# Attention and LoRA feed-forward kernel: the last tile's second half cut into two quarters, and new instruction orders on all engines

## What is computed

```
def fake_quant(x, s, z):                       # to bytes and back
    return (clip(round(x / s + z), 0, 255) - z) * s
x = x + fake_quant(layernorm(x)) @ fake_quant(ctx)
y = layernorm(x)
weights, selected = top_k(y @ gate_w.T, 2)     # of 8 experts
w_full = one_hot(selected) weighted by softmax(weights)
low = einsum(y, lora_A)                        # 8 experts x rank 16
x = x + y @ base_w.T + base_b + 2.0 * einsum(low, lora_B, w_full)
```

## Time and profile before

| | |
|---|---|
| median of three executions | 171.46 us |
| the profiled execution | 171.14 us |
| span of its trace | 168.9 us |
| TensorE matmuls | 801, busy 159.1 us (94%) |
| VectorE, ScalarE, GpSimd busy | 119.2, 91.2, 18.4 us |
| granted TensorE clock, mean | 0.999 of full speed |

### The profile page before, as it was taken

One profiled execution on the slowest core, in us unless ns is written; L12 is line 12 of the kernel. 1 busy time (PEld: TensorE's weight loads), 2 busy tenths in 40 slices (PEclk: granted clock), 3 DMA queues, 4 the chain that ended last, 5 costly groups with the idle time before them and its releaser, 6 DMA issues.

```text
span 168.9 us, 2344 instructions
## 1 busy us (share of the span) xinstructions
PE 159.1 (94%) x801; PEld 119.6 (71%) x801; DVE 119.2 (71%) x290; ACT 91.2 (54%) x140; POOL 18.4 (11%) x40
## 2 busy tenths in 40 slices
PE   5787999999699999999999999999999999999992
PEld 1243435698588888878888767877888888888881
DVE  4887899996699989998799777964388171540212
ACT  3479999758931556804547687437729536000000
POOL 3132222002003000002200230004004000000000
PEclk9999999999999999999999999999999999999999
DMA  4999999999999923303480999994994992300033
GB/s 106 389 417 409 411 408 377 272 339 387 287 349 297 194 95 66 124 0 63 92 157 20 154 192 161 284 247 75 208 157 82 177 276 87 120 8 0 2 124 124
DMA packets 22187, 32.69 MB, mean 193 GB/s; under 512 B 13856, under 2 KB 13856, under 8 KB 22176
## 3 DMA queue, kind: packets, MB, share of 16 engines
q1 hardware_dynamic: 20016, 25.20, 46.2%
q0 software_dynamic: 2016, 7.34, 23.8%
q10 hardware_dynamic: 144, 0.00, 0.0%
HBM read 22.05 MB, written 4.19 MB: 155 GB/s over the span
## 4 chain that ended last, share of the span: by engine, by line
PE 72%; DMA 18%; SPq 4%; ACT 2%; issue 1%; DVE 1%; ACTq 0%
PE ps_even L1051 26%; PE ps_odd L1051 21%; DMA w_raw<-in_w_t 13%; PE ps_att L996 8%; DMA ring<-in_ctx 5%; PE ps_g L1032 5%; PE ps_g L1035 2%; SPq L250 1%; PE ps_t L977 1%; PE ps_even L1094 1%; PE ps_odd L1094 1%; PE ps_even L1093 1%; PE ps_even L1092 1%; PE ps_odd L1093 1%; PE ps_odd L1092 1%
## 5 line engine op out<-in xcount | busy, mean ns | idle before, releaser
L1051 PE MATMUL ps_even<-w_hi,yt 128*128 128x512 f32 x128 | 38.0, 395 | 0.0
L1051 PE MATMUL ps_odd<-w_hi,yt 128*128 128x512 f32 x128 | 37.4, 403 | 0.0
L1051 PEld LDWEIGHTS ps_odd<-w_hi,yt 128*128 128x128 f32 x128 | 24.0, 188 | 5.9 <-issue 0.2
L996 PE MATMUL ps_att<-c,c1t 128*128 128x512 f16 x96 | 27.4, 382 | 0.3 <-DVE c L705 0.3
L1051 PEld LDWEIGHTS ps_even<-w_hi,yt 128*128 128x128 f32 x128 | 23.4, 188 | 4.8
L1032 PE MATMUL ps_g<-ag,yt 128*128 128x272 f32 x64 | 20.8, 364 | 1.6 <-DVE yt L743 1.6
L1051 PE MATMUL ps_even<-w_lo,yt 128*128 128x512 f32 x64 | 20.6, 392 | 0.0
L1051 PE MATMUL ps_odd<-w_lo,yt 128*128 128x512 f32 x64 | 19.9, 394 | 0.0
L1032 PEld LDWEIGHTS ps_g<-ag,yt 128*128 128x128 f32 x64 | 12.1, 189 | 4.6 <-issue 2.0
L435 ACT ACTIVATE qc<-ring,q_in,q_rec 128x1024 uint16<-128x1024 f32 x11 | 13.4, 1234 | 2.1 <-DVE c L705 1.4
L1051 PEld LDWEIGHTS ps_even<-w_lo,yt 128*128 128x128 f32 x64 | 11.9, 188 | 2.6
(11 more groups left out here) (112 smaller groups left out, 257.6 us busy)
## 6 DMA issues: line engine op xcount, KB each, us to landing
ring<-in_ctx SPq DMA_DIRECT2D x12, 512.0 KB, 9.5
w_raw<-in_w_t SPq DMA_DIRECT2D x8, 512.0 KB, 16.1
x_sb<-in_base_b POOLq DMA_DIRECT2D x8, 512.0 KB, 7.7
out_x<-x_sb SPq DMA_DIRECT2D x16, 256.0 KB, 2.5
x_sb<-in_x SPq DMA_DIRECT2D x7, 512.0 KB, 8.6
x_sb<-zfix POOLq DMA_DIRECT2D x6, 512.0 KB, 6.6
x_sb<-in_ctx SPq DMA_DIRECT2D x4, 512.0 KB, 6.8
ag_raw<-in_ag_t SPq DMA_DIRECT2D x1, 544.0 KB, 14.1
```

The source lines that it names most:

```text
L996: ins = pe.matmul(att_bank(t)[h][:, :], c1t[:, t % 4, k, :], c2[:, k, h * HALF:(h + 1) * HALF], start=(k == 0), stop=(k == CT - 1))
L1051: pe.matmul(ffn_bank[t % 2][h][:, :], rows_of(part, t, k), w[:, k, h * HALF:(h + 1) * HALF], start=start, stop=False)
```

## The change

In the last tile (7) the second half of 512 columns becomes two quarters of 256 columns. `last_piece` gives the three pieces: 0 is the first half in `ps_even[0]`, 1 is columns 512 to 767 in `ps_even[1]`, 2 is columns 768 to 1023 in `ps_att[0]`, which attention no longer needs by then. `base_last`, `lora_last`, `finish_last` and `store_last` take the place of the calls for tile 7. A quarter has its own three products per k and three in LoRA: 54 matmuls of 256 columns where 27 of 512 stood, and one finish and one store (128 KB) each.

All lists of calls are new. The most that a reader needs of them:

```
+        LAST = TILES - 1
+        last_piece = [(ps_even[0], 0, HALF), (ps_even[1], HALF, HALF // 2), (ps_att[0], HALF + HALF // 2, HALF // 2)]
...
+            def store_last(p):
+                _bank, a, n = last_piece[p]
+                sp.wait_ge(out_ready, 2 * LAST + p + 1)
+                sp.dma_start(out_d[LAST][:, a:a + n], x_sb[:, LAST, a:a + n]).then_inc(stored, 16)
...
-            load_context(0)
-            load_context(1)
             load_x(1)
-            load_context(2)
-            load_context(3)
+            for k in range(0, 3):
+                load_context(k)
             load_x(2)
...
+            for k in range(6, 9):
+                load_context(k)
+            load_w(0)
+            load_w(1)
+            load_ag()
+            load_w(2)
+            load_w(3)
+            load_context(9)
             load_b()
...
+            load_w(6)
+            load_w(7)
+            load_x(4)
+            load_context(12)
...
+            def finish_last(p):
+                bank, a, n = last_piece[p]
+                if p == 0:
+                    dve.wait_ge(bias_added[LAST], 16)
+                    dve.wait_ge(rowfix_ready, TILES)
+                    dve.wait_ge(ffn_half, TILES)
+                elif p == 1:
+                    dve.wait_ge(ffn_third, 1)
+                else:
+                    dve.wait_ge(ffn_done, TILES)
+                dve.scalar_tensor_tensor(out=x_sb[:, LAST, a:a + n], in0=bank[:, 0:n],
+                                         scalar=rowfix[:, LAST:LAST + 1], in1=x_sb[:, LAST, a:a + n],
+                                         op0=ALU.add, op1=ALU.add).then_inc(out_ready, 1)
...
+            def base_last(p, k):
+                bank, a, n = last_piece[p]
+                if k == 0:
+                    pe.wait_ge(out_ready, 2 * (LAST - 1))
+                    if p == 2:
+                        pe.wait_ge(att_taken, 2 * TILES)
+                if k % 4 == 0:
+                    pe.wait_ge(ylo_ready, 2 * LAST + k // 4 + 1)
+                pe.matmul(bank[:, 0:n], rows_of(0, LAST, k), w_hi[:, k, a:a + n], start=(k == 0), stop=False)
+                pe.matmul(bank[:, 0:n], rows_of(0, LAST, k), w_lo[:, k, a:a + n], start=False, stop=False)
+                pe.matmul(bank[:, 0:n], rows_of(1, LAST, k), w_hi[:, k, a:a + n], start=False, stop=False)
...
+            def lora_last(p):
+                bank, a, n = last_piece[p]
+                pe.wait_ge(ltlo_ready, TILES)
+                pe.matmul(bank[:, 0:n], lt_hi[:, :], b_hi[:, a:a + n], start=False, stop=False)
+                pe.matmul(bank[:, 0:n], lt_hi[:, :], b_lo[:, a:a + n], start=False, stop=False)
+                ins = pe.matmul(bank[:, 0:n], lt_lo[:, :], b_hi[:, a:a + n], start=False, stop=True)
+                ins.then_inc((ffn_half, ffn_third, ffn_done)[p], 1)
```

More of the change, by code:

```diff
@@ L333, in _ @@
             store(6, 1)
-            store(7, 0)
-            store(7, 1)
-            sp.wait_ge(stored, 32 * TILES)
+            for k in range(0, 3):
+                store_last(k)
+            sp.wait_ge(stored, 32 * TILES + 16)
         @block.gpsimd
@@ L1047, in bank_free, with one_pass @@
                         pe.wait_ge(zfix_ready, 4)
-            def one_pass(t, k, part, w, halves, start):
-                for h in halves:
+            def one_pass(t, k, part, w, start):
+                for h in range(2):
                     pe.matmul(ffn_bank[t % 2][h][:, :], rows_of(part, t, k), w[:, k, h * HALF:(h + 1) * HALF],
@@ L1139, in _ @@
                 base_high(0, k)
-            for k in range(0, 7):
+            for k in range(0, 8):
                 low_and_gate(0, k)
@@ L1212, in _ @@
             transpose_low(2)
-            base(3, 2)
-            base(3, 3)
-            lora(2, 0)
-            base(3, 4)
+            for k in range(2, 5):
+                base(3, k)
             low_and_gate(3, 0)
@@ L1253, in _ @@
[L1253 removed]
+            attention(7, 2)
             low_and_gate(4, 5)
[L1255 removed]
+            attention(7, 3)
             low_and_gate(4, 6)
[L1257 removed]
+            attention(7, 4)
             low_and_gate(4, 7)
[L1259 to L1260 removed]
+            for k in range(2, 6):
                 base(4, k)
             transpose_low(4)
[L1263 removed]
+            attention(7, 5)
             base(4, 6)
@@ L1290, in _ @@
-            base(6, 1)
+            lora(5, 1)
+            for k in range(0, 3):
+                base(6, k)
             transpose_low(6)
-            lora(5, 1)
-            for k in range(2, 5):
-                base(6, k)
-            for k in range(0, 8):
+            base(6, 3)
+            base(6, 4)
+            base_last(1, 0)
+            for k in range(0, 3):
                 low_and_gate(7, k)
-            base(7, 0, (0,))
+            base_last(2, 0)
+            low_and_gate(7, 3)
```

415 lines of the change are left out of this document (205 added, 210 removed).

## The result

| | kernel before | changed kernel |
|---|---|---|
| median, us | 171.41 (171.02 to 171.63, 4 runs) | 169.71 (169.46 to 169.86, 4 runs) |
| ratio | | 0.990, 95% interval 0.988 to 0.992 |
| profiled execution, us (span) | 171.14 (168.9) | 169.82 (167.6) |

The changed kernel is 1.70 us faster by the medians and 1.32 by the two profiled executions. A later session gave 170.16 against 171.37, ratio 0.9905 (0.9874 to 0.9937). The forecast was 170.5, with a range of 169.5 to 171.9.

The account below looks back on a forecast made before the run. TensorE's work plus its idle time was taken as the bound. Terms -1.4 + 0.1 + 0.35 + 0.14 + 0 + 0.39 - 0.31 - 0.15 = -0.9 took profiled 171.14 to 170.2; 0.3 more gave median 170.5, range 169.5 to 171.9.

Parts of the forecast that it names:

- Item 1: TensorE's 1.62 us stall at 44 us: earlier ScalarE splits of tile 1 leave 0.2 of it, gain 1.4 us.
- Item 2: First stage: context block 0 lands 1.27 us later but block 7 sets the pace; cost 0.1 us, bounds 0 to 0.3.
- Item 3: Tile 4's gate: less TensorE work covers the exponential, join and split chain; new wait 0.35 us, bounds 0 to 0.9.
- Item 4: Gate steps followed by attention save about 0.035 each; 22 such neighbours instead of 26, cost 0.14 us.
- rival A: Thin places with margins under 1 us, around tiles 4 and 6, eat the gain: 171.1 to 171.3 us; chance 0.25.
- Item 5: Later zero-point add on GpSimd delays SyncE's load of tile 4's x; cost 0, cover about 1 us.
- rival B: Tile 4's x lands too late behind the delayed zero-point add, attention waits 2.3 us: 172.8 us; chance 0.11.
- Item 6: Last tile on TensorE: 54 quarter matmuls at 0.121 for 27 of 512 columns, cost 0.39 us.
- Rival C: Last tile's quarter matmuls are paced by the weight load's 0.19 us each: 174.2 us; chance 0.03.
- Item 7: Kernel end: last finish of 256 columns saves 0.31 us, last store of 128 KB saves 0.15.
- rival D: Quarters nearly free, 0 to 0.07 us, and the stall at 44 us goes whole: 169.9 us; chance 0.12.

Follow-up runs that it names:

- early_split: Kernel before with one ScalarE row moved: the split of tile 1's first half right behind weight block 5's split; 170.11 us, ratio 0.988.
- early_two: Kernel before with two ScalarE rows moved: tile 1's first-half split behind weight block 5's, its second-half split ahead of context block 9's scaling; 169.76 us, ratio 0.988.
- act_back: Changed kernel with ScalarE's splits of tile 1 and first gate exponential put back behind weight blocks 6 and 7 and the zero-point row; 176.31 us, ratio 1.025 to before.
- zfix_back: Changed kernel with GpSimd's zero-point add for tile 3 put back ahead of the bias add; 170.08 us, ratio 0.989 to before.
- q_only: Kernel before with only the last tile's second half in two quarters, nothing else moved; 171.26 us, ratio 0.997.
- cover4: Changed kernel with TensorE's base(3, 6) moved behind the last attention pass of that stretch, under tile 4's gate; 169.39 us, again 169.92, ratios 0.985 and 0.989 to before.
- p384_128: Changed kernel with the last 512 columns cut as 384 and 128 instead of 256 and 256; 170.82 us, ratio 0.995 to before.
- cover5: cover4 with base(3, 5) also moved, ahead of tile 5's first attention pass instead of behind its last; 170.63 us, ratio 0.993 to before.

## Why the forecast came out right

*Item 1, the stall at 44 us (-1.4).* The mechanism holds: early_split and early_two remove it with one and two rows, act_back brings it back. The size was low. I left 0.2 of the stall, and none is left. I had counted block 5 as landing at 38.2 and its split as ending at 39.3; both blocks 4 and 5 had landed when ScalarE reached them (2.00 for both from 34.95, no wait), and what ScalarE then waited for was TensorE. zfix_back gives the reason: with a second zero-point add ahead of the bias add, block 5 is split at 38.28, as I had counted. My "less if only one zfix add competes" was worth over 1 us of landing. And the wait costs more than its idle time: the matmul behind it took 0.36 instead of 0.12. 1.62 + 0.24 = 1.86, and early_two's middle is 1.85 shorter. The stall isn't the same in each execution either: with q_only's 2.20 the same step is worth 0.6 more.

*Item 2, the start (+0.1).* 32.13 against 32.04; the traces vary by 0.9 there, so it is neither shown nor refuted.

*Item 3, tile 4's gate (+0.35).* The place and the cause are right. The trace shows 0.06 of idle and 0.24 in the chain's piece for the gate matmul, 0.30 in all, and cover4 gets 0.2 to 0.3 of it back. My text looked for 0.3 us of idle; most of it stands in that piece, where a look for idle alone would miss it.

*Item 4, neighbours (+0.14).* No run has it apart. What the order costs elsewhere is seen as a whole: the changed kernel without quarters (halves_after) has a middle of 131.95, early_two one of 131.43. The 0.5 between them holds the 0.3 of item 3 and 0.2 that stays without a cause, as large as this item. The 0.16 at tile 5's first pass (0.02 of idle and 0.59 for 0.45), a place that my rival A hadn't named, is in the changed kernel's first trace and not in halves_after. The second trace has none there, but a like wait at the second column sums, which rival A had named. Its chain of waits:

```profile
77.06 0.04 issue
77.11 0.60 PE ps_even L1040 x2
```

In the first trace, in halves_after and in early_two this pair takes 0.45 or 0.46 without a wait, so it is 0.19 here.

*Item 5, GpSimd's and SyncE's lists (0).* Right. Tile 4's first variance starts at 57.67 with no wait for x (57.85 before), so rival B, the slower one, did not happen. zfix_back shows the weights over 1 us later with the old place, and no cost of it that could be timed.

*Item 6, the quarters (+0.39).* 0.119 each instead of 0.121: 54 x 0.119 - 27 x 0.228 = 0.27. The differences of whole middles: 132.42 or 132.52 less 131.95 less 0.11 of bookkeeping is 0.36 to 0.46, q_only 0.34. The first two hold the 0.16 and the 0.19 of item 4. Without these the quarters cost 0.20, 0.27 and 0.34, near the 0.27 of the spacing, so 0.39 was 0.1 too high. Rival C, the weight load's 0.19, is out: p384_128 shows the load's pace at 0.11. The issue gap of the Trainium skill's page "TensorE: Matmul & The Clock Gate" (section Back-to-back issue gap), by which a quarter would be 0.109, is not met: 0.119 is measured at full clock. The page gives that gap for a matmul by itself; for weight load and matmul in a stream it has about 81 ns at 128 columns and 131 at 512, and the traces here have 110 and 228.

*Item 7, the end (-0.46).* Measured -0.53: matmul 0.12, finish 0.27, landing 0.1. The matmul's part is in item 6 already, which counts all 54, so -0.42 stands against my -0.46. The finish took 0.48, not the 0.44 of the line between two rows, and the store saved 0.1, not 0.15. Items 6 and 7 together are nothing, as forecast (-0.07): halves_after and the changed kernel have the same middle plus end.

So the sign and the places were right, and the size was little over half: 1.0 forecast of 1.7. 170.5 was 0.8 too slow. The measured 169.71 is outside the narrower range of the forecast itself (169.9 to 171.0); the wider one, 169.5 to 171.9, holds it because rival D had a place in that. Between the traces I had forecast -0.9, and they differ by -1.32; the 0.4 is about what item 1 lacked (0.2 left over and 0.24 behind the wait). The other 0.4 is the step from a trace to the median. I had added 0.3 because the median of before lies that much above its profiled execution, and the changed kernel's lies 0.1 below its own. Why, no run shows; a stall that was short in the one trace of before would do it. The measured time lies nearest to rival D (169.9), but half of its reason is wrong: the stall went whole, yet the quarters were not free.

## What to carry to other kernels

A list that a planner has rewritten on all engines may owe its gain to two rows. Look for the one wait that ends last, and move what stands ahead of its releaser; here two moved lines of ScalarE gave -1.6 us, act_back shows that the changed kernel needs tile 1's splits early too, and splitting the last tile gave nothing that could be timed. Work that covers one wait is taken from under another (cover5), so before moving a row ask which DMA or add it was hiding. And judge such edits by stretches of the trace that repeat within 0.1 us, not by spans in which the start alone varies by 0.9; see first whether the traced execution is near the median. Where TensorE stalls, look at the granted clock of every execution too, for the stall may cost more than its length in some of them.
